# Causal mask of the first score product of layer 0: added by VectorE with the maxima, with the loop over batches written out

## The chip, the cores and the metric

The kernel runs on one core of a Trainium2 chip. The metric is the time of the device for one execution of the whole program, in microseconds (us), the median of several runs. Times of single instructions come from one execution taken by the hardware profiler. PE is TensorE (PEld its weight load), DVE is VectorE, ACT is ScalarE, POOL is GpSimd, SP is SyncE.

## The reference

Two layers over x of 8 batches x 512 rows x 256 columns. Each adds an attention and a feed-forward branch to x, both fed by the layer norm of x. Only the attention of layer 0 is touched by the change:

```python
xn = _layernorm(x, axis=-1)
c_kv = x @ W_DKV                       # x is xn here, 64 latent columns
k = (c_kv @ W_UK).reshape(b, t, h, hd) # 16 heads of 16
v = (c_kv @ W_UV).reshape(b, t, h, hd)
q = (x @ W_UQ).reshape(b, t, h, hd)
scores = jnp.einsum('bqhd,bkhd->bhqk', q, k) * scale
scores = jnp.where(causal, scores, -inf)
probs = jax.nn.softmax(scores, axis=-1)
ctx = jnp.einsum('bhqk,bkhd->bqhd', probs, v).reshape(b, t, d)
return ctx @ W_O
```

Layer 0's other branch is a gated feed-forward net with 1024 hidden columns and ternary weights; layer 1 has an attention with a position bias and a feed-forward net that selects tokens. They follow in the program and stay as they are.

## The kernel before

**What a batch needs.** The softmax is done with the largest score of each row known in advance. For each pair of heads the scores are therefore computed twice. The *score product* (line 610) has queries on the partitions: for tile t of 128 queries it multiplies with the keys 0 to 128(t+1), at least 256 columns, for two heads at once, each on 64 of the 128 rows of the array. Its output is a double bank of PSUM, one bank a head. VectorE takes the maxima of its rows (line 523, tile `peak`). When the eight score products of a group of four heads are through, the maxima are turned (`maxima`, line 624), copied (line 527) and put by a DMA into the stacks as a further row of the queries. The *prob product* (line 634) then has keys on the partitions and gives score minus maximum; ScalarE takes its exponential (line 411), GpSimd clears what lies above the diagonal of its diagonal block (line 350, `affine_select`), and every second step a *value product* (line 648) adds four heads' probabilities times values into `o_bank`. Layer norm, x turned, latent, q and k, values, and the output product of a batch are spread among these.

**The mask of the score product.** A row's maximum must be taken over the keys that the row may see. Before, two matmuls a head add the mask to the diagonal block of 128 columns (line 615): a product of a bfloat16 selection matrix with a bfloat16 table of 0 and -1e30, one for each half of 64 rows; the second starts at column 64. They are four matmuls a step, 128, 128, 64 and 64 columns wide, behind the score product and ahead of the semaphore `a_ps` that lets VectorE start. The tables come from `half` and are made by one cast of ScalarE (line 372).

**Order of work.** The order is written out in a table: a turn has 32 steps; each has one prob product (of 13 steps earlier in the count) and one score product, and `placed` puts the other events at fixed steps, those of the next batch's layer norm at steps 3 to 11, its transposes of x at 12, latent at 16, q and k at 18 to 22. Each engine emits its own part of that list in that order and waits for semaphores in between. The products take the three double banks `slots` in turn; a product waits until its bank's last reader is through (`claim` with `LAST_READ`: for a score product the maxima, `a_max`; for a prob product the exponential, `p_exp`). So a slow reader on VectorE or ScalarE holds up TensorE two to three products later.

**The loop.** `turns` (line 226) writes out turns -1 and 0, runs turns 1 to 6 in a hardware loop, and writes out turns 7 and 8. In the loop the wait values depend on the counter; they are worked out in registers ahead of each wait, and `hold` adds a semaphore instruction of its own in front of GpSimd's selection, VectorE's aggregation and SyncE's stack loads:

```python
def hold(eng, held, tally, k, b):
    wait(eng, tally, k, b)
    if not isinstance(b, int):
        eng.sem_inc(held.sem, 1)
```

In layer 1 `turns` is written out throughout, and there VectorE adds its bias and takes the maxima in one instruction a head (line 1101), whose result is fetched by a second, short one.

Of the kernel before, what the change touches and what calls it, by code (L numbers as in the profile page):

```python
# [17 lines left out]
BF16 = mybir.dt.bfloat16  # L18
ALU = mybir.AluOpType
ACT = mybir.ActivationFunctionType  # L20
AX_X = mybir.AxisListType.X

P = 128
B, T, D = 8, 512, 256
# [5 lines left out]
HROWS = P // 2  # L30
# [7 lines left out]
NEG = -1.0e30  # L38
# [58 lines left out]
def latent_attention(nc, x_d, out_d, xh_d, xl_d, w, c, sems, front):  # L97
# [4 lines left out]
    with ExitStack() as ctx:  # L102
        def sb(name, shape, dt=F32):
            return ctx.enter_context(nc.sbuf_tensor(f"l0_{name}", shape, dt))
# [3 lines left out]
        def sem(name, per=0, grant=0, unit=1):  # L108
            tallies.append(Tally(sems.enter_context(nc.semaphore(f"l0_{name}")), per, grant, unit))
            return tallies[-1]  # L110
# [1 line left out]
        STEPS, LAG, RING = 32, 13, 4  # L112

        ident, cols, power = sb("ident", [P, P]), sb("cols", [P, 4]), sb("power", [P, TT])
        half, half_b = sb("half", [P, 2, 2, P]), sb("half_b", [P, 2, 2, P], BF16)
        c_low = cols[:, 3:4]

        names = ("q", "k", "v", "c")
# [13 lines left out]
        stacks = sb("stacks", [P, 2, PAIRS, T], F32R)  # L132
        peak, tops = sb("peak", [P, QUADS, 2, 2, TT]), sb("tops", [NE, QUADS, P], F32R)
# [12 lines left out]

        consts_in, masks_in = sem("consts_in", unit=16), sem("masks_in", unit=16)
        w_in = {n: sem(f"w_in_{n}", unit=16) for n in names + ("o",)}
        blank, keyed, ones_ready, half_ready, w_high, w_ready = \
            sem("blank"), sem("keyed", unit=16), sem("ones_ready"), sem("half_ready"), sem("w_high"), sem("w_ready")  # L150
        x_loaded, x_saved = sem("x_loaded", 1, unit=16), sem("x_saved", 2, unit=16)
        stats_done, moments_done, xn_ready = sem("stats_done", TT), sem("moments_done", TT), sem("xn_ready", TT)
        eps_done, rstd_ready = sem("eps_done", 1), sem("rstd_ready", 1)
# [66 lines left out]
        def slot(kind, n):  # L220
            return slots[[(u[0], u[2]) for u in USES].index((kind, n)) % 3]
# [4 lines left out]
        def turns(eng, emit):  # L226
            def turn(i):
                for kind, off, n in STEADY:
                    if there(i + off):
                        emit(kind, i + off, n, i)  # L230
            turn(-1)
            turn(0)
            with eng.Fori(1, B - 1) as i:
                turn(i)
            turn(B - 1)
            turn(B)

        def opening(b):
            return isinstance(b, int) and b == 0
# [4 lines left out]
        def wait(eng, tally, k, b):  # L244
            value = tally.at(k, b)
            if not isinstance(value, int) or value > 0:
                eng.wait_ge(tally.sem, value)
# [7 lines left out]
        def score_of(n):  # L255

            g, pr, t = n // 8, n // 4 % 2, (0, 3, 1, 2)[n % 4]
            return g, pr, t, max((t + 1) * P, MIN_N)
# [16 lines left out]
        def head(a, rows=HROWS):  # L275
            return slice(a * HROWS, a * HROWS + rows)

        with nc.Block() as block:
            @block.sync
            def _(sp):  # L280
# [32 lines left out]
                for name in ("c", "q", "k"):  # L313
                    for dst, src in w["place"](name, raw[name], dict(w["loads"])[name]):
                        sp.dma_start(dst, src).then_inc(w_in[name].sem, 16)
                for dst, src in ((cols, c["c_cols"]), (half, c["c_half"])):
                    sp.dma_start(dst[:], src).then_inc(masks_in.sem, 16)
                for dst, src in w["place"]("v", raw["v"], dict(w["loads"])["v"]):
                    sp.dma_start(dst, src).then_inc(w_in["v"].sem, 16)
# [38 lines left out]
            def _(act):  # L358
# [9 lines left out]
                rounded(wq[:, 0], raw["q"][:])  # L368
                act.wait_ge(w_in["k"].sem, 16 * 2)
                rounded(wk[:, 0], raw["k"][:, 0], HD ** -0.5)  # L370
                act.wait_ge(masks_in.sem, 16 * 2)
                act.copy(half_b[:], half[:]).then_inc(half_ready.sem, 1)

                def more_high_weights():
                    act.wait_ge(w_in["v"].sem, 16 * 2)
# [69 lines left out]
            def _(dve):  # L445
# [18 lines left out]
                def emit(kind, b, n, i):  # L464
# [54 lines left out]
                        dve.tensor_copy(mixt[:, 0], mix_full[:]).then_inc(mh_ready.sem, 1)  # L519
                    if kind == "score":  # L520
                        g, pr, t, wide = score_of(n)
                        wait(dve, a_ps, n + 1, b)
                        dve.tensor_reduce(peak[:, g, :, pr, t], slot(kind, n)[:, :, 0:(t + 1) * P], AX_X, ALU.max)\  # L523
                           .then_inc(a_max.sem, 1)
                    if kind == "maxima":
                        wait(dve, m_ps, n + 1, b)
                        dve.tensor_copy(tops[:, n], m_bank[0:NE, 0:P]).then_inc(tops_ready.sem, 1)
# [21 lines left out]
            def _(pe):  # L549
# [17 lines left out]
                def emit(kind, b, n, i):  # L567
# [31 lines left out]
                    if kind == "score":  # L599

                        g, pr, t, wide = score_of(n)
                        out = claim(kind, n, i)
                        if n % 4 == 0:
                            wait(pe, stack_in[g][pr], 3, b)
                        if n == 0 and opening(b):
                            pe.wait_ge(half_ready.sem, 1)
                        diag = slice(t * P, (t + 1) * P)
                        for a in range(2):
                            r = head(a, HROWS - 1)
                            pe.matmul(out[:, a, 0:wide], stacks[r, 0, 2 * g + pr, diag], stacks[r, 1, 2 * g + pr, 0:wide],  # L610
                                      start=True, stop=False, skip_group_check=True)
                        for part in range(2):
                            for a in range(2):
                                r, first = head(a), part * HROWS
                                ins = pe.matmul(out[:, a, t * P + first:(t + 1) * P], half_b[r, part, 0],  # L615
                                                half_b[r, part, 1, first:P], start=False, stop=part == 1,
                                                skip_group_check=True)
                        ins.then_inc(a_ps.sem, 1)
                    if kind == "maxima":
                        wait(pe, a_max, 8 * n + 8, b)  # L620
# [1878 lines left out]
```

## Time and profile before

| what | value |
|---|---|
| median of three runs | 1964.74 us (1958.15 to 1965.31) |
| profiled execution | 1956.55 us |
| its span | 1954.7 us |
| PE busy in the span | 1730.8 us, 89%, 11015 matmuls |
| DVE busy | 1151.7 us, 59%, 2519 instructions |
| ACT busy | 1064.3 us, 54% |
| POOL busy | 976.0 us, 50% |
| reductions of line 523 | 206.2 us in 256 instructions, mean 822 ns |

The span runs from the first to the last instruction of the program; the device's time has 1.85 us more around it. Busy time is the union of an engine's instructions; matmuls are pipelined and their ends are modelled, so start-to-start distances say more about TensorE than lengths. A timeline row gives start, length and instruction, with how many like it were merged, and in brackets how long the engine was idle before it and what ended that.

### The profile page before, as it was taken

Reading aid. Unit: us, or ns where it says so; the run is one execution under the profiler, and the core shown is the slowest. Engines: PE = TensorE matmul, PEld = TensorE weight load, DVE = VectorE, ACT = ScalarE, POOL = GpSimd, SP = SyncE. Lnnn points to the kernel's source line nnn. Section 1 sums busy time; section 2 is a strip of 40 time slices with the busy share of each in tenths; the row PEclk is TensorE's granted clock in tenths of the full one; section 3 lists DMA queues with packets and bytes.
Section 4 is the critical chain, followed back from the end, with each engine's and each line's share of the span. In section 5 each row is a group of like instructions: output and inputs, shape, how many; then the busy total and the mean of one; then the engine's idle time right before and its main releaser. Section 6 shows DMA issues by size and latency. Waiting matters only on the chain. (4 is left out here: it accounts for less than half of the span.)

```text
span 1954.7 us, 32406 instructions
## 1 busy us (share of the span) xinstructions
PE 1730.8 (89%) x11015; PEld 1130.8 (58%) x11015; DVE 1151.7 (59%) x2519; ACT 1064.3 (54%) x1471; POOL 976.0 (50%) x735
## 2 busy tenths in 40 slices
PE   4989888887999999999999967788888888878998
PEld 3455554544788888888888754343333333326565
DVE  6665566653343533435335438988888888846345
ACT  2555555555632323223223325989888889885643
POOL 2344444432334444344433435877787787884202
PEclk7899999998999999999999976999998999998999
DMA  4333233322531201112011172322322223117357
GB/s 128 88 106 94 81 97 96 104 76 92 193 96 37 84 24 59 56 35 75 24 59 61 35 269 68 80 84 76 88 76 79 85 76 93 49 58 253 121 153 230
DMA packets 119262, 182.86 MB, mean 94 GB/s; under 512 B 14197, under 2 KB 73077, under 8 KB 119162
## 3 DMA queue, kind: packets, MB, share of 16 engines
q1 hardware_dynamic: 112812, 173.21, 29.0%
q10 hardware_dynamic: 5712, 6.29, 1.1%
q0 software_dynamic: 640, 2.10, 0.3%
q8 instruction: 56, 0.92, 0.2%
q14 instruction: 42, 0.34, 0.1%
HBM read 90.72 MB, written 39.91 MB: 67 GB/s over the span
## 5 line engine op out<-in xcount | busy, mean ns | idle before, releaser
L878 POOL TENSOR_TENSOR l_prob<-l_prob,l_bias 128x1024 f32<-128x1024 f32 x192 | 453.1, 2381 | 104.8 <-ACT l_prob L1035 103.4
L1326 POOL TENSOR_TENSOR f_hl<-f_full,f_hh 128x512 fp32r<-128x512 f32 x192 | 248.2, 1293 | 401.1 <-DVE f_hh L1364 273.3
L1101 DVE CUSTOM_DVE_ANT_0 l_slot<-l_slot,l_bias 128x512 f32<-128x512 f32 x512 | 340.0, 714 | 28.8 <-PE l_slot L1186 28.7
L1038 ACT ACTIVATE l_prob<-l_prob 128x1024 f32<-128x1024 f32 x256 | 273.5, 1075 | 0.0
L523 DVE TENSOR_REDUCE l_peak<-l_slot 128x2 f32<-128x256 f32 (+3 forms) x256 | 206.2, 822 | 108.5 <-PE l_slot L615 105.4
L1414 PE MATMUL f_ps<-f_hh,f_hi_h 128*128 128x512 f32 x1024 | 260.6, 390 | 3.3 <-ACT f_hh L1338 2.7
L1414 PE MATMUL f_ps<-f_hl,f_hi_h 128*128 128x512 f32 x1024 | 258.3, 389 | 0.0
L411 ACT ACTIVATE l_prob<-l_slot 128x1024 f32<-128x1024 f32 (+3 forms) x256 | 175.3, 706 | 96.9 <-PE l_slot L634 93.9
L1414 PEld LDWEIGHTS f_ps<-f_hh,f_hi_h 128*128 128x128 f32 x1024 | 191.9, 188 | 47.4 <-issue 3.4
L1346 ACT ACTIVATE f_full<-f_ps,f_h_s 128x512 f32<-128x512 f32 x128 | 87.0, 685 | 236.3 <-PE f_ps L1414 217.4
L1414 PEld LDWEIGHTS f_ps<-f_hl,f_hi_h 128*128 128x128 f32 x1024 | 192.2, 188 | 39.9
L1364 DVE CAST f_hh<-f_full 128x512 fp32r<-128x512 f32 x128 | 62.2, 486 | 257.0 <-ACT f_full L1346 257.0
L350 POOL TENSOR_SCALAR_AFFINE_SELECT l_prob<-l_prob 128x256 f32<-128x256 f32 x256 | 105.9, 421 | 210.8 <-ACT l_prob L411 208.3
L1035 ACT COPY l_prob<-l_slot 128x1024 f32<-128x1024 f32 x192 | 195.3, 1017 | 16.9 <-PE l_slot L1202 16.3
L1186 PE MATMUL l_slot<-l_stacks 63*128 63x512 f32 x512 | 119.4, 467 | 63.2 <-DVE l_prob L878 30.9
L1216 PE MATMUL l_o_bank<-l_prob,l_vals 128*32 128x512 f32 x1024 | 143.8, 635 | 8.4 <-ACT l_prob L1038 5.2
L1202 PE MATMUL l_slot<-l_stacks 64*128 64x512 f32 x512 | 129.3, 505 | 16.3 <-DVE l_peak L1101 15.5
L610 PE MATMUL l_slot<-l_stacks 63*128 63x256 f32 (+2 forms) x512 | 98.8, 382 | 27.0 <-ACT l_prob L411 16.2
L634 PE MATMUL l_slot<-l_stacks 64*128 64x256 f32 (+2 forms) x512 | 110.1, 429 | 10.5 <-DVE l_peak L523 4.1
L1186 PEld LDWEIGHTS l_slot<-l_stacks 63*128 63x128 f32 x512 | 51.2, 198 | 103.4 <-DVE l_prob L878 47.3
L1202 PEld LDWEIGHTS l_slot<-l_stacks 64*128 64x128 f32 x512 | 50.0, 193 | 103.6 <-DVE l_peak L1101 68.9
L648 PE MATMUL l_o_bank<-l_prob,l_vals 128*32 128x512 f32 (+3 forms) x1024 | 98.1, 455 | 11.1 <-POOL l_prob L350 9.7
(230 smaller groups left out, 2795.7 us busy)
## 6 DMA issues: line engine op xcount, KB each, us to landing
l_stacks<-l_parts SPq DMA_DIRECT2D x372, 128.0 KB, 2.6
f_raw<-in_L_ffn_h_w SPq DMA_DIRECT2D x16, 512.0 KB, 4.1
f_raw<-in_L_ffn_h_w SPq DMA_DIRECT2D x32, 256.0 KB, 2.6
e_w<-in_L_ffn_f SPq DMA_DIRECT2D x32, 256.0 KB, 3.0
l_bias<-ext SPq DMA_DIRECT2D x16, 448.0 KB, 8.0
attn<-l_out_sb ACTq DMA_DIRECT2D x9, 512.0 KB, 2.9
l_x_in<-in_L_attn_x SPq DMA_DIRECT2D x8, 512.0 KB, 3.9
xh<-l_xh SPq DMA_DIRECT2D x8, 512.0 KB, 2.6
```

The costliest lines, as they stand in the source:

```text
L411: act.activation(prob[:, n // 2 % RING, 2 * pr:2 * pr + 2, j * P:T], slot(kind, n)[:, :, j * P - q0:wide], ACT.Exp).then_inc(p_exp.sem, 1)
L523: dve.tensor_reduce(peak[:, g, :, pr, t], slot(kind, n)[:, :, 0:(t + 1) * P], AX_X, ALU.max)\
L634: ins = pe.matmul(out[:, a, 0:wide], stacks[r, 1, 2 * g + pr, j * P:(j + 1) * P], stacks[r, 0, 2 * g + pr, q0:T], start=True, stop=True)
L878: return eng.tensor_tensor(probs(n), src, bias[:, h:h + 2, j * P:j * P + T], ALU.add)
L1035: act.copy(probs(n), slot(kind, n)[:]).then_inc(p_copied.sem, 1)
L1038: act.activation(probs(n), probs(n), ACT.Exp).then_inc(p_exp.sem, 1)
L1101: ins = dve.tensor_tensor_reduce(src, src, bias[:, 4 * g + 2 * pr + a, t * P:t * P + T], 1.0, 3 * NEG, ALU.add, ALU.max, peak[:, g, a, pr, ...
L1186: ins = pe.matmul(out[:, a], stacks[r, 0, 2 * g + pr, t * P:(t + 1) * P], stacks[r, 1, 2 * g + pr, ::-1], start=True, stop=True)
L1202: ins = pe.matmul(out[:, a], stacks[r, 1, 2 * g + pr, j * P:(j + 1) * P], stacks[r, 0, 2 * g + pr, ::-1], start=True, stop=True)
L1216: ins = pe.matmul(o_bank[32 * a:32 * a + 32, :], vals_sb[:, v0:v0 + 32], prob[:, n % RING, a], start=(j == 0), stop=(j == TT - 1), skip_gr ...
L1326: pool.tensor_tensor(t.hl[layer % 2][:, o], t.full[:, n % 2], t.hh[layer % 2][:, o].bitcast(F32), ALU.subtract).then_inc(self.h_lo.sem, 1)
L1414: ins = pe.matmul(t.hidden[n % 4][:], t.hi[m][:, k, cut], src[layer % 2][:, k], start=first and k == 0, stop=last and k == KH - 1, skip_gr ...
```

## The change

Three things change, all in the attention of layer 0.

1. The score product is two matmuls with nothing behind them; the four mask matmuls, the tables `half` and `half_b`, their cast on ScalarE and the wait for it are gone.
2. VectorE reads a mask of 128 x 512, zero but for the last 128 columns, which hold the causal triangle. For each of the two heads one instruction adds its last 128(t+1) columns to the scores, writes the sum back to PSUM and takes the row's maximum. A short instruction fetches that maximum, and the last of these signals `a_max`.
3. `turns` is written out for all ten turns.

```diff
-        half, half_b = sb("half", [P, 2, 2, P]), sb("half_b", [P, 2, 2, P], BF16)
+        mask = sb("mask", [P, T])
...
-            turn(-1)
-            turn(0)
-            with eng.Fori(1, B - 1) as i:
+            for i in range(-1, B + 1):
                 turn(i)
-            turn(B - 1)
-            turn(B)
...
-                for dst, src in ((cols, c["c_cols"]), (half, c["c_half"])):
+                for dst, src in ((cols, c["c_cols"]), (mask, c["c_mask"])):
...
-                act.wait_ge(masks_in.sem, 16 * 2)
-                act.copy(half_b[:], half[:]).then_inc(half_ready.sem, 1)
...
+                        if n == 0 and opening(b):
+                            dve.wait_ge(masks_in.sem, 16 * 2)
                         wait(dve, a_ps, n + 1, b)
-                        dve.tensor_reduce(peak[:, g, :, pr, t], slot(kind, n)[:, :, 0:(t + 1) * P], AX_X, ALU.max)\
-                           .then_inc(a_max.sem, 1)
+                        for a in range(2):
+                            src = slot(kind, n)[:, a, 0:(t + 1) * P]
+                            ins = dve.tensor_tensor_reduce(src, src, mask[:, T - (t + 1) * P:T], 1.0, 3 * NEG,
+                                                           ALU.add, ALU.max, peak[:, g, a, pr, t:t + 1])
+                        ins.then_inc(a_max.sem, 1)
...
-                        if n == 0 and opening(b):
-                            pe.wait_ge(half_ready.sem, 1)
-                        diag = slice(t * P, (t + 1) * P)
                         for a in range(2):
                             r = head(a, HROWS - 1)
-                            pe.matmul(out[:, a, 0:wide], stacks[r, 0, 2 * g + pr, diag], stacks[r, 1, 2 * g + pr, 0:wide],
-                                      start=True, stop=False, skip_group_check=True)
-                        for part in range(2):
-                            for a in range(2):
-                                r, first = head(a), part * HROWS
-                                ins = pe.matmul(out[:, a, t * P + first:(t + 1) * P], half_b[r, part, 0],
-                                                half_b[r, part, 1, first:P], start=False, stop=part == 1,
-                                                skip_group_check=True)
+                            ins = pe.matmul(out[:, a, 0:wide], stacks[r, 0, 2 * g + pr, t * P:(t + 1) * P],
+                                            stacks[r, 1, 2 * g + pr, 0:wide], start=True, stop=True)
                         ins.then_inc(a_ps.sem, 1)
```

TensorE in the middle of a turn, two steps of a group, before (610 is the score product, 615 its mask, 634 the prob product, 648 the value product, 247 register arithmetic for a wait):

```order
L634 MATMUL l_slot<-l_stacks 128x256 x2
L247 REGISTER_ALU
L610 MATMUL l_slot<-l_stacks 128x384 x2
L615 MATMUL l_slot<-l_half_b 128x128 x2
L615 MATMUL l_slot<-l_half_b 128x64 x2
L247 REGISTER_ALU
L634 MATMUL l_slot<-l_stacks 128x256 x2
L247 REGISTER_ALU
L610 MATMUL l_slot<-l_stacks 128x256 x2
L615 MATMUL l_slot<-l_half_b 128x128 x2
L615 MATMUL l_slot<-l_half_b 128x64 x2
L648 MATMUL l_o_bank<-l_prob,l_vals 32x256 x4
```

And of the change (606 is the score product now, 624 the prob and 638 the value product):

```order
L624 MATMUL l_slot<-l_stacks 128x256 x2
L606 MATMUL l_slot<-l_stacks 128x384 x2
L624 MATMUL l_slot<-l_stacks 128x256 x2
L606 MATMUL l_slot<-l_stacks 128x256 x2
L638 MATMUL l_o_bank<-l_prob,l_vals 32x256 x4
```

The order of the products is the same; masks and register arithmetic are gone from between them.

VectorE in the next batch's layer norm, before (468, 472 and 474 belong to the norm):

```order
L523 TENSOR_REDUCE l_peak<-l_slot 128x2
L468 BN_STATS l_stats<-l_x_in 128x6
L247 ISA
L472 BN_AGGR l_moments<-l_stats 128x2
L247 REGISTER_ALU
```

And of the change, the same place (521 is the add with maximum and the read of its result):

```order
L521 ISA l_slot,l_peak<-l_slot,l_mask 128x512
L521 ISA l_peak 128x1
L521 ISA l_slot,l_peak<-l_slot,l_mask 128x512
L521 ISA l_peak 128x1
L462 BN_STATS l_stats<-l_x_in 128x6
L466 BN_AGGR l_moments<-l_stats 128x2 x4
```

Four instructions stand where one stood, at the same place among those of the norm.

ScalarE's exponentials in the loop, before, with the semaphores that each waits for:

```order
L247 REGISTER_ALU [waits l0_b_ps]
L411 ACTIVATE l_prob<-l_slot 128x1024 [waits l0_value_ps]
L247 REGISTER_ALU
L411 ACTIVATE l_prob<-l_slot 128x1024 [waits l0_b_ps]
L247 REGISTER_ALU
L247 ISA [waits l0_value_ps]
L421 COPY l_o_sb<-l_o_bank 128x512 [waits l0_ot_ps]
```

And of the change (405 is the exponential, 415 the copy of `o_bank`):

```order
L405 ACTIVATE l_prob<-l_slot 128x1024 [waits l0_value_ps,l0_b_ps]
L405 ACTIVATE l_prob<-l_slot 128x1024 [waits l0_b_ps]
L415 COPY l_o_sb<-l_o_bank 128x512 [waits l0_ot_ps,l0_value_ps]
L405 ACTIVATE l_prob<-l_slot 128x2x384 [waits l0_value_ps,l0_b_ps]
L405 ACTIVATE l_prob<-l_slot 128x2x384 [waits l0_b_ps]
```

The register instruction that stood between the two waits of the first of a pair is gone.

## Rows read from the trace of the kernel before

**Rows 1.** Busy time by stretch: engines' us, granted clock, DMA share, GB/s.
```profile
30.00:50.00 20.00, 15.63 (x109) 10.45 (x105) 15.24 (x30) 3.06 (x3) 4.10 (x4) 0.50 0.34 100
63.00:80.00 17.00, 14.27 (x141) 7.46 (x141) 10.21 (x14) 10.17 (x14) 7.44 (x13) 0.90 0.33 81
305.17:317.30 12.13, 10.50 (x121) 5.11 (x119) 11.20 (x24) 6.78 (x12) 5.00 (x11) 1.00 0.28 70
319.00:355.00 36.00, 31.71 (x306) 19.31 (x304) 19.32 (x30) 20.30 (x28) 16.84 (x22) 1.00 0.33 98
```

**Rows 2.** Line 404, ScalarE's copy of the values, whole run.
```profile
L404 ACT COPY l_vals<-l_slot x8: 1012/1014/1022, 50.3 to 432.3; 128x1024 f32<-128x1024 f32 x8
```

**Rows 3.** Timeline of TensorE, turn 5: start us, us, instruction [idle before].
```profile
304.40 0.39 PE L634 MATMUL l_slot<-l_stacks 64*128 64x256 f32 x2
304.62 0.40 PE L610 MATMUL l_slot<-l_stacks 63*128 63x512 f32 x2
304.86 0.26 PE L615 MATMUL l_slot<-l_half_b 64*128 64x128 bf16 x4
304.96 0.37 PE L634 MATMUL l_slot<-l_stacks 64*128 64x256 f32 x2
305.56 0.38 PE L610 MATMUL l_slot<-l_stacks 63*128 63x256 f32 x2 [0.23 <-ACT l_prob L411]
305.79 0.26 PE L615 MATMUL l_slot<-l_half_b 64*128 64x128 bf16 x4
305.98 0.85 PE L648 MATMUL l_o_bank<-l_prob,l_vals 128*32 128x384 f32 x8
```

**Rows 4.** Timeline of ScalarE, the same stretch.
```profile
304.91 1.09 ACT L411 ACTIVATE l_prob<-l_slot 128x512 f32<-128x512 f32 x2 [1.01 <-PE l_slot L634]
```

**Rows 5.** Timelines of VectorE and TensorE where VectorE is waited for.
```profile
305.17 1.82 DVE L523 TENSOR_REDUCE l_peak<-l_slot 128x2 f32<-128x1024 f32 x2 [0.38 <-PE l_slot L615]
...
311.57 0.69 DVE L523 TENSOR_REDUCE l_peak<-l_slot 128x2 f32<-128x512 f32 x1
...
312.32 0.44 PE L634 MATMUL l_slot<-l_stacks 64*128 64x384 f32 x2 [0.46 <-DVE l_peak L523]
...
317.76 0.44 PE L573 MATMUL l_slot<-l_ident,l_xn 128*128 128x128 f32 x2 [0.28 <-DVE l_xn L477]
```

**Rows 6.** Groups by shape, line 523, 301 to 355 us: count | busy us, mean ns.
```profile
L523 DVE TENSOR_REDUCE l_peak<-l_slot 128x2 f32<-128x512 f32 x9 | 6.2, 689 | 1.0 <-PE l_slot L615 0.7
L523 DVE TENSOR_REDUCE l_peak<-l_slot 128x2 f32<-128x256 f32 x8 | 3.3, 417 | 2.7 <-PE l_slot L615 2.7
```

**Rows 7.** Timeline of VectorE in layer 1: the add-and-maximum and its read.
```profile
1402.28 0.73 DVE L1101 CUSTOM_DVE_ANT_0 l_slot<-l_slot,l_bias 128x512 f32<-128x512 f32 x1
1402.92 0.14 DVE L1101 DVE_READ_ACCUMULATOR2_ANT l_peak<- 128x1 f32 x1
```

**Rows 8.** Timelines of TensorE and ScalarE, in the loop, then in turn 7.
```profile
348.29 0.39 PE L634 MATMUL l_slot<-l_stacks 64*128 64x256 f32 x2
...
348.79 1.09 ACT L411 ACTIVATE l_prob<-l_slot 128x512 f32<-128x512 f32 x2 [0.42 <-PE l_slot L634]
...
452.06 0.39 PE L634 MATMUL l_slot<-l_stacks 64*128 64x256 f32 x2
...
452.49 0.60 ACT L411 ACTIVATE l_prob<-l_slot 128x512 f32<-128x512 f32 x1 [0.34 <-PE l_slot L634]
```

**Rows 9.** Timelines of GpSimd and TensorE behind the layer norm.
```profile
320.86 2.36 POOL L337 TENSOR_TENSOR l_xl<-l_x_full,l_xh 128x1024 fp32r<-128x1024 f32 x1 [2.66 <-DVE l_xh L490]
...
323.63 0.42 PE L648 MATMUL l_o_bank<-l_prob,l_vals 128*32 128x128 f32 x8 [1.34 <-POOL l_prob L350]
```

**Rows 10.** Timeline of TensorE across a jump back, and where the loop ends.
```profile
300.02 0.39 PE L610 MATMUL l_slot<-l_stacks 63*128 63x256 f32 x2 [0.54 <-ACT l_prob L411]
...
408.39 0.39 PE L610 MATMUL l_slot<-l_stacks 63*128 63x256 f32 x2 [0.54 <-ACT l_prob L411]
...
412.82 0.39 PE L634 MATMUL l_slot<-l_stacks 64*128 64x256 f32 x2
```

More of the change, by code:

```diff
@@ L148, in latent_attention @@
         w_in = {n: sem(f"w_in_{n}", unit=16) for n in names + ("o",)}
-        blank, keyed, ones_ready, half_ready, w_high, w_ready = \
-            sem("blank"), sem("keyed", unit=16), sem("ones_ready"), sem("half_ready"), sem("w_high"), sem("w_ready")
+        blank, keyed, ones_ready, w_high, w_ready = \
+            sem("blank"), sem("keyed", unit=16), sem("ones_ready"), sem("w_high"), sem("w_ready")
         x_loaded, x_saved = sem("x_loaded", 1, unit=16), sem("x_saved", 2, unit=16)
```

## The prediction

> **What bounds the kernel now.** I read the stretches first, then one turn of the loop instruction by instruction. The layer 0 attention fills about 30 to 490 us of the span of 1954.7 us, one turn for each of 8 batches, 54.6 us a turn (ScalarE's copy of the values starts 8 times between 50.3 and 432.3 us) [rows 2]. Nothing after it is touched. In a turn at full clock TensorE is busy 88% (31.71 of 36 us), yet this is no engine that never waits. VectorE is at 54% there, but at 92% between 305.17 and 317.30 us, where the next batch's layer norm lies among the maxima [rows 1].
>
> The unit to look at is a pair of steps, since a value product comes every second step. The three double banks of PSUM go round among the products: the score product at 305.56 waits 0.23 us for a bank, that of the prob product at 304.40, which ScalarE has been reading since 304.91 [rows 3, 4]. So the chain of a pair is: score product, its mask, value product, prob product, exponential, next score product. The second mask of the pair (304.86, followed by a prob product at 304.96) lies beside ScalarE's exponential and is paid by nobody as long as that wait is there. Where VectorE is late, its maxima hold the bank instead: the prob product at 312.32 waits 0.46 us for the reduction begun at 311.57, and the transposes of x at 317.76 wait 0.28 us for the last normalized tile [rows 5].
>
> **The change, part by part.**
> *Masks off TensorE.* Four matmuls a step go. They are 0.26 us long, but two rows of the array run side by side and the next product starts 0.10 us after them (304.86 to 304.96) or 0.19 us (305.79 to 305.98) where a full-array product follows [rows 3]; the difference of 0.09 is that product's weight load, which follows the score product just as well. I take 0.10 us a step, bounds 0.10 and 0.19. VectorE also starts 0.10 us earlier. Only masks ahead of a value product (16 of 32 in a turn) are surely on the chain: 1.6 us a turn, and 3.2 us if all were.
>
> *Maxima on VectorE.* One reduction over both heads becomes two add-and-maximum instructions, each with a read of its result. The same pair of operations runs in layer 1: the add starts at 1402.28, its read at 1402.92, together with the next add, so 0.64 us for 512 columns, and the read ends 0.14 later [rows 7]. A reduction over 2x512 followed by another takes 1.82-0.69 = 1.13 us from start to start [rows 5, 6]. The price is 2x0.64-1.13 = +0.15 us a step. Reductions grow by (689-417)/256 = 1.06 ns an element [rows 6]; so 0.54 of the 0.64 us are elements and 0.10 is fixed. Layer 1 has no such instruction below 512 columns. For 128 to 384 columns I take the same fixed 0.10, hence +0.15 at every width, since nothing in the row depends on width but the elements; the upper bound is that any width takes 0.64 us, which against a mean reduction of 0.73 us start to start gives +0.55 a step; the lower is a fixed part hidden as in the reduction, 0.
>
> Where does it fall? Between 305.17 and 317.30 there are ten score steps, so 10x0.15 = 1.5 us of new work. The first begins 0.10 earlier. The stretch has 0.93 us idle [rows 1] in four gaps, and as instructions in a row overlap by about 0.08 us, it can take in 0.93+4x0.08 = 1.25. What is left makes the last normalized tile, and with it the transposes of x at 317.76, **late by 0.2 us**, and the six masks' gain ahead of them is lost. That lateness is handed on without cover: transposes, ScalarE's copy, VectorE's cast, GpSimd's subtraction (2.36 us from 320.86) and the value product at 323.63, which already waits 1.34 us for it [rows 9]. From there to the next layer norm VectorE has room: nine masks stand ahead of a value product, 0.9 us, of which VectorE's longer chain (512, 256, 384, 128 columns from 349 us on) takes back some 0.1.
>
> *Loop written out.* In the loop an instruction that waits twice has register arithmetic between the waits. At 348.29 to 348.79 the exponential starts 0.50 us after its product; in the last turn, which is written out already, 452.06 to 452.49 is 0.43 [rows 8]. Where that instruction is the one being waited for, 0.07 goes; outside the norm's stretch I count four such places a turn, on ScalarE and on TensorE behind a copy of ScalarE: 0.3 us. On GpSimd the extra semaphore instruction goes too; I cost that at nothing, as its result is wanted four steps later, except behind the subtraction above, where it is hidden under 2.36 us of work. The same holds for SyncE: its stack transfers are issued several steps ahead, and no product waits for them.
>
> The jump back itself: TensorE goes from 300.02 to 304.40 through the branch in 4.38 us, and from 408.39 to 412.82 where the loop is left in 4.43 [rows 10]. By the rows it is free. The Trainium skill, "Runtime: NRT & Kernel Launch", section on instruction fetch mechanics, says that a taken branch to a page not held stops the engine for a fetch, and that written-out code streams; by it the six jumps would be a gain that my sum lacks. The trace does not agree for TensorE. Scalar preparation of the half masks (one cast of ScalarE) is off the path, and the mask's transfer is as large as the old one: nothing.
>
> **Sum.** Turns 1 to 6: +0.2-0.8-0.3 = -0.9 us each, -5.4. Turn 7 has no layer norm and no loop: -1.1 (its masks ahead of value products, less one). Turn 0: ten steps with a layer norm and little else, where TensorE has half its clock (0.50 of full, so 1.2 GHz) and VectorE 15.2 of 20 us [rows 1]; +1.5, less 0.2 of earlier start and 0.1 of gaps, and -0.9 in its rest: +0.3. Together **-6 us**. The profiled execution took 1956.55 us, so 1950.5 by it; it was faster than the median of the three runs, 1964.74, which gives **1958.7**.
>
> **The rivals.**
> *A, TensorE really is the bound.* VectorE's gaps take all in, and the value masks all count: -1.6-0.6 = -2.2 us a turn in six turns and -1.5 in the other two, -16 us, 1948.5; with every mask on the chain, -3.2-0.6 in six turns and -3 in two, -29 us, 1936. For it speaks TensorE's busy share; against it the wait of 0.46 us for VectorE [rows 5] and the 92%. Chance 0.23, nearly all of it at the smaller gain.
> *B, VectorE becomes the bound: slower.* Place: the narrow add-and-maximum instructions in the norm's stretch. With x us added a step the lateness is 10x-1.35, against -1.1 elsewhere, so it turns at x = 0.25. At x = 0.45 it is +3.2-1.1 = +2.1 a turn and, with turn 0 slower by 3, about +14 us, 1979; at the bound of 0.55, +3.1 a turn, 1988. For it: no narrow one is in the trace. Against: BN and reductions beside them scale plainly. Chance 0.12.
> *C, the clock.* From 63 to 80 us the granted clock is 0.90 of full [rows 1]: 3.4 of 17 us at 1.2 GHz, in a stretch where TensorE was busy 14.3 us, and such drops cost at most half their length, 1.7 us. With fewer matmuls there may be more of them; one more a turn is up to +12, so 1971 at worst, some 1965 likely. The Trainium skill's page "TensorE: Matmul & The Clock Gate", part 1, makes the clock follow the array's activity; by that rule taking matmuls out can lower it. The rows show drops, not what a mask's worth of activity does. Chance 0.10.
> *D, jumps do cost,* on an engine that I could not compare: the 0.54 us that TensorE waits for ScalarE before the branch [rows 10] would be the most a turn, -3 us more, 1955.5. Chance 0.03.
> *E, neither part matters:* TensorE's gain is all met by VectorE: 1964 to 1965. Chance 0.07.
>
> **How the numbers follow.** My forecast, 1954 to 1962, has 0.45. The measurement of this kernel tells about 0.5% from no change, 9.8 us. Faster by over that, below 1955: most of A, a corner of the forecast and of D, and the spread of the runs (1958.15 to 1965.31), 0.31. Slower, above 1974.5: B and the worst of C, 0.14. The rest, 0.55, is the same. The range takes the smaller form of A with the runs' spread, 1945, and reaches towards B and past C, 1972; the far ends of A and B are left out.
>
> **What would show it.** In the profile after: TensorE's busy share of a stretch down by its masks, score-to-value distance 0.32 instead of 0.41 us; an add of 128 columns followed by its read after some 0.24 us (B: 0.4 or more); VectorE nearly without gaps in the norm's stretch, and the transposes of x waiting for it by more than 0.28 us (A: less); exponentials 0.43 us behind their 256-column products everywhere; the values' copy every 53.5 us or so (A: 52 to 52.5, B: 56). If the copies come 1 us or more closer than now, I was wrong about VectorE's cover; if no closer, about the masks on the chain.

## The result, and the profile after

The changed kernel took 1973.92 us in the median (1965.03 to 1975.22, six runs) against 1964.84 us (1958.15 to 1967.76, six runs) for the kernel before on the same chip: ratio 1.0048, 95% interval 1.0030 to 1.0066. The forecast was 1958.7 us, 6 us faster, with a range up to 1972; the kernel is 9 us slower, just outside that range. A second measurement of the same kernel beside other runs gave 1977.87 us, ratio 1.0088 [1.0065, 1.0110]. The profiled execution took 1973.07 us.

The page of the changed kernel; the last two rows give line, engine, shapes and count, then busy time and mean ns, then the engine's idle time before them.

```profile
span 1971.4 us, 29672 instructions
...
PE 1717.5 (87%) x9991; PEld 1109.7 (56%) x9991; DVE 1187.4 (60%) x3287; ACT 1062.6 (54%) x1470; POOL 977.2 (50%) x735
...
L521 DVE CUSTOM_DVE_ANT_0 l_slot<-l_slot,l_mask 128x128 f32<-128x128 f32 (+3 forms) x512 | 238.0, 517 | 89.8 <-PE l_slot L606 88.3
...
L624 PE MATMUL l_slot<-l_stacks 64*128 64x256 f32 (+2 forms) x512 | 110.4, 430 | 19.3 <-DVE l_peak L521 10.7
```

1024 masks are gone, yet TensorE is busy for 1717.5 us instead of 1730.8. Of the idle time ahead of the prob products 10.7 us now end with VectorE's maxima; in the kernel before it was 4.1 us:

```profile
L634 PE MATMUL l_slot<-l_stacks 64*128 64x256 f32 (+2 forms) x512 | 110.1, 429 | 10.5 <-DVE l_peak L523 4.1
```

ScalarE's copy of the values marks the turns; it started from 50.3 to 432.3 us before [rows 2], and now:

```profile
L398 ACT COPY l_vals<-l_slot x8: 1013/1018/1022, 51.7 to 444.8; 128x1024 f32<-128x1024 f32 x8
```

Seven turns took 393.1 instead of 382.0 us, 11.1 us of the 16.7 by which the two spans differ; the last value product of layer 0 starts 14.6 us later (487.6 instead of 473.0). So nearly all of the loss lies in the attention of layer 0. The turns differ among themselves, though, and what they follow is the clock. Busy time by turn, first of the kernel before, then of the changed one; the clock stands before the DMA share:

```profile
159.50:215.20 55.70, 49.92 (x476) 29.70 (x476) 34.83 (x62) 29.93 (x44) 23.48 (x37) 0.96 0.34 97
...
271.00:325.20 54.20, 47.95 (x476) 28.05 (x476) 34.83 (x62) 29.88 (x43) 23.48 (x37) 1.00 0.34 97
```

```profile
108.50:163.80 55.30, 46.54 (x348) 24.89 (x350) 39.24 (x158) 29.87 (x44) 23.75 (x37) 0.96 0.32 93
...
332.30:391.30 59.00, 51.14 (x348) 28.67 (x348) 39.35 (x158) 29.61 (x43) 23.75 (x37) 0.88 0.34 92
```

At a clock of 0.96 a turn took 55.7 us before, and the changed kernel's three take 55.3 to 56.0; at 0.88 it takes 59.0. Two quantities are therefore kept apart below. **Time at half clock** (1.2 GHz) of a run is 2 x (1 - its mean granted clock) x its span, averaged over the timed runs. **A turn at full clock** (2.4 GHz) comes from a line laid through turns 2 to 6 of all 14 profiles of this case (70 turns, one slope, a height for each kernel): 0.30 us for each us at half clock, with a residue of 0.27 us. The heights are good to 0.15 to 0.2 us each. For the changed kernel the height is where the line leads, since none of its five turns had the full clock throughout.

| kernel | median us | ratio [95%] | half clock, us a run | turn at full clock |
|---|---|---|---|---|
| before (67 runs) | 1961.6 | 1 | 184 | 54.3 |
| changed, first / again | 1973.9 / 1977.9 | 1.0048 / 1.0088 | 217 / 245 | 54.3 / 54.2 |
| 1 before, written out | 1956.4 | 0.9963 [0.9945, 0.9981] | 179 | 53.9 |
| 2 changed, in the loop | 1984.4 | 1.0118 [1.0085, 1.0151] | 240 | 55.1 |
| 3 both masks, written out | 1969.2 | 1.0033 [1.0017, 1.0049] | 186 | 55.6 |
| 4 neither mask, written out | 1948.3 | 0.9941 [0.9915, 0.9967] | 195 | 52.6 |
| 5 changed + wide off-chain matmuls | 1956.3 | 0.9977 [0.9960, 0.9994] | 178 | 54.0 |
| 6 kernel 4 + wide ones | 1945.6 | 0.9917 [0.9901, 0.9933] | 170 | 52.6 |
| 7 changed, light in the norm | 1957.9 | 0.9980 [0.9963, 0.9997] | 200 | 53.4 |
| 8 changed, light elsewhere | 1966.9 | 1.0033 [1.0016, 1.0051] | 225 | 53.5 |
| 9 masks split between engines | 1965.5 | 1.0019 [1.0004, 1.0034] | 209 | 53.6 |
| 10 kernel 1 + wide ones | 1952.6 | 0.9959 [0.9942, 0.9975] | 166 | 54.0 |
| 11 changed + thin ones | 1970.9 | 1.0045 [1.0028, 1.0063] | 220 | 54.1 |

So at equal clock the change does nothing that can be seen, 54.3 to 54.3 us a turn, where -0.9 was forecast; and it runs 33 to 61 us longer at half clock, which at 0.30 is 10 to 18 us. In the two profiles the seven turns have 26 us at half clock before and 64 us after, the rest of the program 154 and 151 us: the longer half clock, too, lies in layer 0's turns.

The two quantities account for every row: seven times the difference in the turn, plus 0.30 times the difference in time at half clock, gives each kernel's ratio to the kernel before within 3.3 us. The 0.30 holds without the turns as well: among the timed runs of one and the same kernel (169 runs), a us more at half clock goes with 0.28 us more of time.

### The profile page after: what moved, and what is told of

Read it like the earlier page. It is cut to its first block and busy times, and to the rows that moved or that the text cites. A ratio compares the mean times of both kernels' runs of the same rounds, so it can differ in the third digit from the quotient of the medians.

```text
span 1971.4 us, 29672 instructions
## 1 busy us (share of the span) xinstructions
PE 1717.5 (87%) x9991; PEld 1109.7 (56%) x9991; DVE 1187.4 (60%) x3287; ACT 1062.6 (54%) x1470; POOL 977.2 (50%) x735
## 5 line engine op out<-in xcount | busy, mean ns | idle before, releaser
L521 DVE CUSTOM_DVE_ANT_0 l_slot<-l_slot,l_mask 128x128 f32<-128x128 f32 (+3 forms) x512 | 238.0, 517 | 89.8 <-PE l_slot L606 88.3
L624 PE MATMUL l_slot<-l_stacks 64*128 64x256 f32 (+2 forms) x512 | 110.4, 430 | 19.3 <-DVE l_peak L521 10.7
```

Of the source, the lines that this page charges most:

```text
L521: ins = dve.tensor_tensor_reduce(src, src, mask[:, T - (t + 1) * P:T], 1.0, 3 * NEG, ALU.add, ALU.max, peak[:, g, a, pr, t:t + 1])
L624: ins = pe.matmul(out[:, a, 0:wide], stacks[r, 1, 2 * g + pr, j * P:(j + 1) * P], stacks[r, 0, 2 * g + pr, q0:T], start=True, stop=True)
```

## Experiments

### The parts, one by one

Kernel 1 is the kernel before with `turns` written out:

```diff
-            turn(-1)
-            turn(0)
-            with eng.Fori(1, B - 1) as i:
+            for i in range(-1, B + 1):
                 turn(i)
-            turn(B - 1)
-            turn(B)
```

> The kernel before with the loop written out and nothing else changed (masks on TensorE, one reduction on VectorE). Clock theory and VectorE theory alike: the two-wait instructions lose 0.07 us, so 1 to 3 us faster than before, with half-clock time between 60 and 470 us near the 27 us of before. Rival (the written-out loop is what costs): most of the 9 us, 5 to 10 us slower than before.

It took 1956.4 us, 7 us under the kernel before on its chip (1963.4). The turn went from 54.3 to 53.9 us, -0.4, and the six looped turns give -2.4; the clock gives 5 x 0.30 = -1.5. The sum, -3.9, lies within the interval (-3.7 to -10.8 us). That is faster than the 1 to 3 us of either theory, and clearly against the rival. What the other 3 us are, no row says; kernels 3 and 4, measured beside the same runs of the kernel before, come out 3 us below what turn and clock give them as well, and kernel 10, also written out but measured elsewhere, 0.5 us, so they may belong to the comparison and not to the loop.

Kernel 2 is the changed kernel with that edit reversed, and with VectorE's wait for a score product as a semaphore instruction of its own (`hold`), so it has a little more in the loop than the mere reversal would.

> The changed kernel with the hardware loop kept: mask and maxima on VectorE, turns 1 to 6 looped. Clock and VectorE theories: as slow as the change or up to 3 us slower, so 9 to 12 us over before. Loop rival: back to within 3 us of before.

1984.4 us, 23 us over the kernel before by the ratio and slower than either theory allowed; the loop rival is out. A turn is 55.1 us: the loop costs more here, 0.8 us a turn, than on the kernel before. The extra instruction on the now busier VectorE is in that figure. The rest of the 23 us is time at half clock, 240 us a run.

Kernel 3 keeps the mask matmuls, written out, and has VectorE's add with maximum too (the mask is added twice, harmlessly):

```diff
-                        dve.tensor_reduce(peak[:, g, :, pr, t], slot(kind, n)[:, :, 0:(t + 1) * P], AX_X, ALU.max)\
-                           .then_inc(a_max.sem, 1)
+                        for a in range(2):
+                            src = slot(kind, n)[:, a, 0:(t + 1) * P]
+                            ins = dve.tensor_tensor_reduce(src, src, mask[:, T - (t + 1) * P:T], 1.0, 3 * NEG,
+                                                           ALU.add, ALU.max, peak[:, g, a, pr, t:t + 1])
+                        ins.then_inc(a_max.sem, 1)
```

> Written out, the mask added twice: by TensorE's four matmuls as before and again by VectorE with the maxima (the sum is still far below 3e30; the maxima are the same). Clock theory: TensorE keeps its work, so half-clock time falls back near 27 us and the time is only 1 to 4 us over before, several us below the change. VectorE theory: VectorE's chain is as long as in the change and TensorE's longer by its masks, so 10 to 14 us over before.

It came out between the two theories, 6.5 us over the kernel before by the ratio (3 to 10): the clock is back at 186 us at half clock as the one said, and the turn is the longest of all written-out kernels, 55.6 us, as the other said.

Kernel 4 is the changed kernel with the minus lines of this diff in place of its plus lines:

> Written out, no mask in the maxima at all: score product, then one plain reduction over the same columns; a row's subtracted value is then the largest over its whole diagonal block, and the masking of the probabilities is unchanged. VectorE theory: the masks' gain comes without the price, 8 to 16 us faster than before. Clock theory: half-clock time is as in the change (60 us between 60 and 470 us), which eats most of it: 0 to 5 us faster than before, or none.

1948.3 us is 12 us under the kernel before by the ratio (6.5 to 17), what the VectorE theory said; of the clock theory's loss there is little, 195 us at half clock.

Together these two close a square of four written-out kernels. At full clock:

| turn, us | masks on TensorE | no masks on TensorE | difference |
|---|---|---|---|
| plain reduction | 53.9 | 52.6 | -1.3 |
| add with maximum | 55.6 | 54.3 | -1.3 |
| difference | +1.7 | +1.7 | |

**Over a whole turn the two parts add up**, as far as heights good to 0.2 us can tell: taking the masks from TensorE gives 1.3 us a turn whatever VectorE does, and VectorE's longer work costs 1.7 us whatever TensorE does. The changed kernel is nevertheless 3 to 11 us above kernel 3 by the ratios and not 8 x 1.3 = 10 us below. The column "half clock" has most of the rest: 179 and 186 us a run with masks on TensorE, 195 and 217 to 245 without. Here the parts do not add up: VectorE's longer work alone brings 7 us more at half clock, the missing masks alone 16, both together 38 to 66.

What VectorE's price is made of, TensorE's prob products of one turn show, first of the changed kernel, then of kernel 4 (idle time before them at the end of the row):

```profile
L624 PE MATMUL l_slot<-l_stacks 64*128 64x256 f32 (+2 forms) x66 | 14.0, 419 | 2.6 <-DVE l_peak L521 1.9 <-ACT l_qk_full L391 0.4
```

```profile
L621 PE MATMUL l_slot<-l_stacks 64*128 64x256 f32 (+2 forms) x66 | 13.9, 417 | 1.4 <-DVE l_peak L519 0.8 <-ACT l_qk_full L391 0.4
```

The waits for the maxima rise by 1.1 us of the 1.7.

### Where VectorE's price is paid

Kernels 7 and 8 are the changed kernel with the plain reduction, without mask, at ten of the 32 score steps or at the other 22:

```diff
+                        if 2 <= n <= 11:
+                            dve.tensor_reduce(peak[:, g, :, pr, t], slot(kind, n)[:, :, 0:(t + 1) * P], AX_X, ALU.max)\
+                               .then_inc(a_max.sem, 1)
+                            return
                         for a in range(2):
```

(kernel 8 has `if not 2 <= n <= 11`).

> The changed kernel, with VectorE's maxima as one plain reduction, without the mask, at the ten score steps 2 to 11 of each turn, where the next batch's layer norm lies; the mask is left out of the maxima there. Theory (the price of the longer VectorE instructions is paid in the norm's stretch): most of the 15 us at equal clock, and of the clock's 7, between the changed kernel and the one without any mask come back: 1952 to 1958. Rival (they are paid for everywhere): 10 of 32 steps' worth, -7 us: 1965 to 1969.

> The complement of the kernel before: plain reductions without the mask at the 22 score steps outside 2 to 11, the add with maximum at the ten steps in the norm's stretch. Theory (the norm's stretch pays): little comes back, 1967 to 1973. Rival (they are paid for everywhere): 22 of 32 steps' worth, -15 us: 1957 to 1961.

Kernel 7's turn at full clock is 0.9 us shorter than the changed kernel's, kernel 8's 0.75 us; together nearly the 1.7 us. A step in the norm's stretch costs 0.09 us, one elsewhere 0.03.

The norm's stretch can also be read directly. From the first prob product behind the turned maxima to the transposes of x, a stretch at full clock takes the same time in every turn of a kernel to within 0.03 us: 13.36 us in the kernel before (304.40 to 317.76), 13.25 in kernel 1, 14.06 in kernel 3, 12.84 in kernel 4, 13.86 in the changed kernel (310.58 to 324.44), 12.84 in kernel 7, 13.69 in kernel 8. So VectorE's longer work costs 1.0 us there without the masks (0.8 with them), all of it paid back by kernel 7, and the other 0.7 of the 1.7 us fall in the rest of the turn. Taking the masks away gains 0.4 us there with plain maxima and 0.2 with the long ones.

My theory was right that the norm's stretch is the dearer place by far, wrong that the rest is free: nearly half of the price lies in the 22 steps that I had given cover. The medians don't show this by themselves (1957.9 and 1966.9), because kernel 8 ran 25 us longer at half clock than kernel 7. Kernel 7's median is just inside the theory's range, kernel 8's just below it.

Kernel 9 was meant to use this: masks on TensorE with plain reductions in the norm's stretch, VectorE's mask at the other 22 steps.

```diff
-                        for part in range(2):
+                        for part in range(2 if 2 <= n <= 11 else 0):
```

> Written out; masks on TensorE with one plain reduction at steps 2 to 11, on VectorE by the add with maximum at the other 22. Theory (VectorE is crowded only in the norm's stretch, TensorE's masks are paid for outside it): faster than either kernel with its loop written out: 1946 to 1954, VectorE's cover kept, and some 22/32 of the 8 to 12 us that the masks cost TensorE gained on the 1956.4 of the loop written out. Rival (paid for everywhere alike): 1956 + 22/32 of (-12 +15) = 1958 to 1961.

1965.5 us, a clear miss: slower than kernel 1, and above the rival's range too. At full clock it behaves as the parts say: 53.9 - 22/32 x 1.3 + 0.75 = 53.75, measured 53.6. But its time at half clock is 209 us against kernel 1's 179, 30 x 0.30 = 9 us, as much as the medians differ. What moving masks about gains in a turn is tenths of a microsecond; what it does to the clock is worth more.

### The clock

In the changed kernel the clock falls behind a stretch in which TensorE waited twice, just after the wait of 1.01 us for the transposes of x. Busy time by stretch, then its timeline in the first of them:

```profile
324.40:331.00 6.60, 4.34 (x39) 2.65 (x40) 4.21 (x17) 3.65 (x5) 3.44 (x4) 1.00 0.25 104
331.00:334.50 3.50, 3.33 (x17) 2.60 (x16) 1.14 (x4) 2.01 (x3) 0.41 (x1) 0.51 0.94 241
```

```profile
327.92 0.50 PE L624 MATMUL l_slot<-l_stacks 64*128 64x512 f32 x2 [0.52 <-DVE l_peak L521]
328.25 0.35 PE L606 MATMUL l_slot<-l_stacks 63*128 63x256 f32 x2
330.21 0.43 PE L638 MATMUL l_o_bank<-l_prob,l_vals 128*32 128x128 f32 x8 [1.61 <-POOL l_prob L346]
330.56 1.66 PE L563 MATMUL l_slot<-l_wv,l_cs 128*128 128x256 f32 x8
```

TensorE was busy 4.34 of 6.60 us with the clock at 1.00; then it is 0.51, and TensorE needs 3.33 of 3.50 us for what comes. The clock falls once more in this turn, at 351.5 us, behind waits of 0.44 and 0.43 us between 348 and 350.

Kernel 5 is the changed kernel, given matmuls that nobody reads or waits for, behind the prob product of every eighth step (the table `half_b` is made again for them; it stands in for nothing else):

```diff
                         ins.then_inc(b_ps.sem, 1)
+                        for m in range({1: 8}.get(n % 8, 0)):
+                            pe.matmul(m_bank[:, 2 * P:3 * P], half_b[:, m % 2, 0], half_b[:, m % 2, 1],
+                                      start=True, stop=True, skip_group_check=True)
```

> The changed kernel with eight small bfloat16 matmuls (128 columns, full array) added behind the prob product of every eighth step, into a part of a bank that nobody reads; nothing waits for them. Clock theory (the masks that left TensorE were also activity; without them its clock is halved for longer): time at half clock, 217 us a run in the changed kernel by its mean granted clock, falls to about 185, what the kernels with masks on TensorE have; at 0.34 us a us that is -11 us, less up to 0.45 us for each of the four groups a turn where they delay a product (32 groups, at most +14): 1962 to 1974, and layer 0's turns at the same clock longer than the changed kernel's by 0 to 1.8 us. Rival (the half clock has nothing to do with the masks): time at half clock stays near 217, and the time is 1974 to 1988.

**1956.3 us: work was added to TensorE, and the program became faster**, by 17.6 us in the medians (14 to 22 us by the ratios to the kernel before on each chip). Time at half clock fell from 217 (245 again) to 178 us. Against their mean of 231, 53 x 0.30 = 16 us, which is the gain within 2 us. The time is below even the clock theory's range: its allowance for delayed products was not needed. The same turn, in its profile; the eight matmuls stand between the two waits:

```profile
319.23 0.51 PE L630 MATMUL l_slot<-l_stacks 64*128 64x512 f32 x2 [0.52 <-DVE l_peak L525]
319.66 0.62 PE L634 MATMUL l_m_bank<-l_half_b 128*128 128x128 bf16 x8
320.21 0.39 PE L612 MATMUL l_slot<-l_stacks 63*128 63x256 f32 x2
321.52 0.43 PE L647 MATMUL l_o_bank<-l_prob,l_vals 128*32 128x128 f32 x8 [0.92 <-POOL l_prob L348]
321.87 1.21 PE L567 MATMUL l_slot<-l_wv,l_cs 128*128 128x256 f32 x8
```

From prob to value product it is 2.29 us in either kernel (319.23 to 321.52, 327.92 to 330.21): the added matmuls lie inside the wait for GpSimd, now 0.92 instead of 1.61 us. The values' products behind it take 1.21 instead of 1.66 us: the clock stayed up. Three turns in a row are then alike, such as

```profile
215.20:269.20 54.00, 46.78 (x380) 26.13 (x382) 39.41 (x158) 29.89 (x44) 23.76 (x37) 1.00 0.36 99
```

The four groups a turn hold TensorE for some 2.2 us (4 x 0.55, from 319.66 to 320.21), and the turn at full clock did not grow: they fall into gaps.

Is it the array's work, or the pause and the shifted phase? Kernel 11 has the same matmuls, 4 columns wide instead of 128:

```diff
-                            pe.matmul(m_bank[:, 2 * P:3 * P], half_b[:, m % 2, 0], half_b[:, m % 2, 1],
+                            pe.matmul(m_bank[:, 2 * P:2 * P + 4], half_b[:, m % 2, 0], half_b[:, m % 2, 1, 0:4],
```

> Off-chain matmuls as in the run before (eight behind every eighth prob product), but 4 columns wide instead of 128: as many instructions, hardly any work of the array. Clock theory (it is the array's work that keeps the clock): like the changed kernel, about 215 us at half clock and 1968 to 1975 us. Rival (the gain came of the pause or the shifted order, not of the array's work): like the wide ones, 178 us at half clock and 1954 to 1959.

1970.9 us and 220 us at half clock, like the changed kernel. The order is the same in both and the pause not far apart: the score product behind the added matmuls starts 0.72 us after the prob product with the thin ones, 0.98 with the wide ones, 0.33 with none. Nor do the wide ones shift the turn: at full clock the transposes of x start 13.86 us and the values' products 19.98 us behind the first prob product behind the turned maxima, in kernels 5 and 11 and in the changed kernel alike, to 0.01 us. So it is the array's work. (Kernels 5 and 11 were measured on different chips; the kernel before had 183 and 185 us at half clock on them.) The changed kernel itself, with no edit, beside it:

> The changed kernel itself, once more beside the kernels of this call, for its spread and for the clock of many runs. Any theory: ratio to the kernel before within 1.003 to 1.0066 as at first, mean granted clock 0.940 to 0.952, so about 215 us at half clock.

Its ratio, 1.0088, misses the expected interval, its granted clock (mean 0.938) the lower end of what was expected; its turn at full clock is 54.2 us, as at first. Both times differ by the clock, and the loss of the change is uncertain by as much: 0.5% to 0.9%.

Kernels 10 and 6 give the same wide matmuls to kernels 1 and 4.

> The kernel before with its loop written out, masks on TensorE, plus the same off-chain matmuls of 128 columns. If the masks' work is what the change lost and there is nothing more to win, half clock stays near 179 us and the time rises by their cost, 1957 to 1964. If the clock can be had still longer also here, half clock falls below 170 and the time to 1950 to 1956.

> No masks on TensorE, plain reductions on VectorE (the maxima leave the mask out), and the off-chain matmuls. Without them it took 1948.3 us with 195 us at half clock. Clock theory: half clock to about 178 us, -6 us, less up to some us for the added matmuls: 1940 to 1948, the fastest of all. Rival: nothing gained from the clock, 1948 to 1958.

By the clock both gained: kernel 10, 1952.6 us, has 166 us at half clock where kernel 1 has 179, the second of its two cases; kernel 6, 1945.6 us, has 170 where kernel 4 has 195. In the time the gain is small, 13 x 0.30 = 4 and 25 x 0.30 = 8 us by the slope, and the ratios don't settle it: 0.9959 beside kernel 1's 0.9963, and 0.9917 beside kernel 4's 0.9941 with intervals that overlap. In the profile of kernel 10, taken of its fastest execution (1946.8 us), the clock is full from the first copy of the values to the last:

```profile
51.20:422.50 371.30, 342.32 (x3497) 202.70 (x3496) 238.44 (x415) 207.56 (x298) 160.18 (x256) 1.00 0.36 97
```

So the masks held up the clock only in part, and it can be held up further. Kernel 10 keeps every mask of the kernel before and is faster than it and than the changed one; kernel 1 is so too, with no added work. Kernel 6 is the fastest, 16 us under the kernel before. Like kernel 4 its maximum runs also over keys that a row may not see; the selection of GpSimd clears their probabilities in any case, but with other data a far larger hidden score would press a row's probabilities towards zero, so kernels 1 and 10 are the ones that do what the kernel before does for any data.

## Why the prediction was wrong

**Price of an add with maximum: right.** The prediction had a fixed part of 0.10 us at every width against rival B. In the changed kernel, by shape, 276 to 332 us (busy us, mean ns):

```profile
L521 DVE CUSTOM_DVE_ANT_0 l_slot<-l_slot,l_mask 128x512 f32<-128x512 f32 x16 | 10.8, 714 | 4.0 <-PE l_slot L606 4.0
...
L521 DVE CUSTOM_DVE_ANT_0 l_slot<-l_slot,l_mask 128x128 f32<-128x128 f32 x16 | 4.4, 316 | 2.6 <-PE l_slot L606 2.6
```

(714-316)/384 = 1.04 ns an element, and 384 and 256 columns (582 and 455 ns) lie on the same line. From start to start it is 0.65 us at 512 columns (311.85 to 312.50) and 0.25 at 128 (315.12 to 315.37), so the fixed part is 0.12 us at both; rival B's narrow floor is not there. VectorE's turn grew from 34.8 to 39.3 us, 0.14 us a step for the 0.15 forecast.

**Where it falls: the step that failed at full clock.** The prediction let the norm's stretch swallow 1.25 of 1.5 us, which with the masks' gain lost there left +0.2 us, and it gave +0.1 us to the other 22 steps, where "VectorE has room". The lateness is there, and larger:

```profile
310.58 0.39 PE L624 MATMUL l_slot<-l_stacks 64*128 64x256 f32 x2
...
318.69 0.45 PE L624 MATMUL l_slot<-l_stacks 64*128 64x384 f32 x2 [0.92 <-DVE l_peak L521]
...
324.44 0.95 PE L572 MATMUL l_slot<-l_ident,l_xn 128*128 128x128 f32 x7 [1.01 <-DVE l_xn L471]
```

The transposes of x wait 1.01 us for 0.28 before, the prob product 0.92 for 0.46 [rows 5]. TensorE reaches the transposes 13.86 us behind the first of these products, for 13.36 us before (304.40 to 317.76): +0.5 us where +0.2 was forecast, masks and loop included. The larger miss is the rest of the turn: at full clock the whole turn changed by 0.0, so the rest gained 0.5 us instead of the 1.1 forecast. The masks and the loop gained there about what they were given, 1.1 and 0.3 us for 0.9 and 0.3; VectorE's longer work took some 0.7 us (1.7 less 1.0) for 0.1. (These three leave a gain of 0.7 and not 0.5, within what the heights allow.) The likely reason, argued from the order and not tested by a run of its own: an instruction that waits for the next score product starts no sooner because there was a gap before it, so when VectorE is late by 0.15 us, a product can wait at once. Summing up the idle time of a stretch bounds what it can take in; it doesn't say that it will.

One count in the sum is off besides: turn 7 is given -1.1 us for its masks ahead of value products less one, which at 0.10 us each would be -1.5. It changes the sum by 0.4 us and nothing in the account.

**Masks off TensorE: right.** 0.10 us each on 16 places, less those of the norm's stretch, was the term; -1.3 us a turn was measured, with either kind of maxima, between my 0.9 and the full 1.6. In the norm's stretch 0.2 of the masks' gain was kept where the prediction had it lost. **Loop written out: right**, -0.4 for -0.3. In the changed kernel too, exponentials stand 0.43 us behind their 256-column products (321.12 behind 320.69 us). That 0.4 us a turn would include a cost of the jump back; rows 10 show none on TensorE.

**The clock: the step that failed in the sum, and the larger error.** Rival C had the mechanism and nearly the size, up to 12 us in all and 1971 us at worst, and got a chance of 0.10. The sum itself went by one clock for both kernels: the term was put at nothing, though the kernel before showed that its clock already fell now and then, 0.90 of full in one stretch [rows 1] and five of its seven turns below full. The norm's lateness and the missing masks both thin out TensorE's work; it took both for the loss to be large. Measured are 33 to 61 us more at half clock, 10 to 18 us. The Trainium skill, "TensorE: Matmul & The Clock Gate", part 1, makes the clock follow the array's activity; the runs agree: same instructions, same places, 128 columns wide 178 us at half clock, 4 columns wide 220 us. Without this term the change would have come out at about nothing, rival E's 1964 to 1965, and not at my -6 either.

Rival A falls with VectorE's price, and for rival D no row shows a cost of the jumps. The test that the prediction set was itself flawed: copies no closer than before were to convict the masks on the chain, but these held, and it was VectorE's cover that failed.

What stays open: why the changed kernel's clock differs so much between two measurements (217 and 245 us, single runs 188 to 274), why late maxima and missing masks together cost so much more clock than each alone, and what of the gain of kernel 1 lies beyond its turns.

## What to carry to other kernels

Read the granted clock turn by turn before costing an edit to a busy TensorE: where some turns are below full, "fewer matmuls" and "a longer wait" both have a second price. Compare versions at equal clock first, then ask what each does to the clock; a few matmuls that nobody waits for, ahead of the longest wait, are a cheap test of it and may be the better change. When work is added to an engine that alternates with another, charge it in full unless a row shows the cover instruction by instruction.

## What the runs showed of the hardware that was not expected

- 32 matmuls a turn of 128 columns, 0.62 us for eight, took the time at half clock from 217 or 245 us down to 178 us a run and cost nothing at full clock (54.0 us a turn); 4 columns wide they left it at 220 us.
- A us at half clock cost 0.30 us in these turns, where TensorE also waits, and not the 0.5 us that halving the speed of unbroken work would cost.
- Waiting twice costs different amounts in the loop: in the kernel before, ScalarE's exponentials that wait twice start 0.11 to 0.12 us behind the end of their product in the loop, where register arithmetic stands between the two waits (348.79 behind 348.68), and 0.04 us in the turns that are written out (452.49 behind 452.45) and in kernel 1. GpSimd's selections, with `hold`'s extra instruction ahead of them in the loop, start 0.16 us behind their exponential there and 0.07 us in those turns.
